# First product copied inside PSUM and the second added to it by TensorE, in a Strassen-Winograd feed-forward stage

## The reference

```python
def reference(x, ctx_1024, g_xattn, g_ffn, Wq, bq, Wk, bk, W_up, W_gate, W_down):
    # _layernorm: (x - mean) / sqrt(var + 1e-5)
    query = einsum('bnc,dc->bnd', ctx_1024, Wq) + bq
    key = einsum('bnc,dc->bnd', ctx_1024, Wk) + bk
    attention = softmax(einsum('bnd,bmd->bnm', query, key))
    x = x + tanh(g_xattn[0]) * einsum('bln,bmn->blm', _layernorm(x), attention)
    # ternary(w): s = mean(|w|) + 1e-8; clip(round(w / s), -1, 1) * s
    wu, wg, wd = ternary(W_up), ternary(W_gate), ternary(W_down)
    n = _layernorm(x)
    hidden = silu(einsum('bsd,ed->bse', n, wu)) * einsum('bsd,ed->bse', n, wg)
    return x + tanh(g_ffn[0]) * einsum('bse,de->bsd', hidden, wd)
```

## Time and profile before

| what | value |
|---|---|
| median of 3 runs | 394.66 us (394.34 to 394.94) |
| span of the profiled execution | 393.2 us |
| median less that span | 1.46 us |
| granted TensorE clock, mean of the span | 1.000 |
| PE busy | 388.2 us (99%), 2000 matmuls |
| DVE busy | 330.2 us (84%) |
| ACT busy | 269.8 us (69%) |
| POOL busy | 183.9 us (47%) |

### The profile page before, as it was taken

One profiled execution on the slowest core, in us unless ns is written; L12 is line 12 of the kernel. 1 busy time (PEld: TensorE's weight loads), 2 busy tenths in 40 slices (PEclk: granted clock), 3 DMA queues, 4 the chain that ended last, 5 costly groups with the idle time before them and its releaser, 6 DMA issues.

```text
span 393.2 us, 6214 instructions
## 1 busy us (share of the span) xinstructions
PE 388.2 (99%) x2000; PEld 219.3 (56%) x2000; DVE 330.2 (84%) x501; ACT 269.8 (69%) x366; POOL 183.9 (47%) x199
## 2 busy tenths in 40 slices
PE   8999999999999999999999999999999999999997
PEld 6676775554444444444444444556545665656886
DVE  0778897988799975789888979999999989798974
ACT  3887988899777786869897982856287566564400
POOL 0498727767845031403169462643639447261000
DMA  8999977799600030020029470006230000000014
GB/s 287 404 402 407 408 232 184 176 261 183 160 2 0 1 108 0 13 96 0 2 60 190 86 148 2 0 1 214 78 139 0 2 1 2 0 2 1 2 61 154
DMA packets 44048, 43.91 MB, mean 112 GB/s; under 512 B 30833, under 2 KB 33009, under 8 KB 42993
## 3 DMA queue, kind: packets, MB, share of 16 engines
q1 hardware_dynamic: 44016, 43.53, 36.3%
HBM read 29.89 MB, written 6.29 MB: 92 GB/s over the span
## 4 chain that ended last, share of the span: by engine, by line
PE 84%; DVE 6%; ACT 4%; issue 4%; DMA 1%; POOL 1%; DVEq 0%; ACTq 0%; POOLq 0%
PE pair L924 20%; PE pair L926 20%; PE pair L1052 14%; PE pair L1000 8%; PE pair L815 7%; PE pair L838 6%; PE pair L788 4%; PE pair L772 3%; PE pair L799 2%; DVE x_sb L1855 1%; DVE xf L1804 1%; DMA xf<-in_first 1%; PE pair L853 1%; DVE sh L1814 1%; ACT xf L1395 1%
## 5 line engine op out<-in xcount | busy, mean ns | idle before, releaser
L924 PE MATMUL pair<-xb_hi,w_sb 128*128 128x512 f16 x448 | 169.8, 379 | 0.9 <-DVE xf L1799 0.5
L926 PE MATMUL pair<-xb_lo,w_sb 128*128 128x512 f16 x448 | 169.8, 379 | 0.0
L924 PEld LDWEIGHTS pair<-xb_hi,w_sb 128*128 128x128 fp8e4 x448 | 43.8, 98 | 54.0 <-DVE xf L1799 1.3
L926 PEld LDWEIGHTS pair<-xb_lo,w_sb 128*128 128x128 fp8e4 x448 | 43.8, 98 | 49.5 <-issue 0.3
L1344 ACT ACTIVATE xf<-xf,small 128x512 f32<-128x512 f32 x48 | 34.5, 720 | 43.5 <-DVE xf L1799 23.6
L1804 DVE SCALAR_TENSOR_TENSOR xf<-xf,small 128x512 f32<-128x512 f32 x48 | 41.7, 870 | 8.5 <-ACT xf L1344 8.4
L1855 DVE SCALAR_TENSOR_TENSOR x_sb<-pair,small,x_sb 128x256 f32<-128x256 f32 (+1 forms) x85 | 37.4, 472 | 6.3 <-PE pair L1052 5.8
L1000 PE MATMUL pair<-x_sb,sh 128*128 128x512 bf16 x192 | 42.4, 379 | 0.0
L626 POOL TENSOR_TENSOR w_sb<-w_sb 128x512 fp8e4<-128x512 fp8e4 x8 | 8.8, 1101 | 55.1 <-ACT w_sb L1215 55.1
L1000 PEld LDWEIGHTS pair<-x_sb,sh 128*128 128x128 f16 x192 | 18.8, 98 | 22.6 <-DVE x_sb L1839 0.2
L1809 DVE TENSOR_TENSOR sh<-xf,sh 128x512 f16<-128x512 f32 x34 | 30.6, 906 | 0.9 <-ACT sh L1357 0.8
(11 more groups left out here) (207 smaller groups left out, 769.2 us busy)
## 6 DMA issues: line engine op xcount, KB each, us to landing
w_sb<-in_wugT SPq DMA_DIRECT2D x8, 1024.0 KB, 14.9
x_sb<-in_x SPq DMA_DIRECT2D x4, 1024.0 KB, 12.8
xf<-in_wdT SPq DMA_DIRECT2D x4, 1024.0 KB, 7.5
xt_sb<-in_wdT SPq DMA_DIRECT2D x4, 1024.0 KB, 4.9
xt_sb<-in_xT SPq DMA_DIRECT2D x12, 256.0 KB, 5.8
x_dram<-x_sb SPq DMA_DIRECT2D x8, 256.0 KB, 3.5
out<-x_sb SPq DMA_DIRECT2D x8, 256.0 KB, 4.2
x_sb<-x_dram SPq DMA_DIRECT2D x4, 512.0 KB, 3.9
```

The lines of the kernel that those rows point to most:

```text
L924: pe.matmul(dst[:, m * 512:(m + 1) * 512], w[:, o:o + P], hi[:, k], start=start and k == 0, stop=False, skip_group_check=not start)
L926: last = pe.matmul(dst[:, m * 512:(m + 1) * 512], w[:, o:o + P], lo[:, k], start=False, stop=k == 1, skip_group_check=not start)
```

## The change

- Product 2 no longer starts a fresh accumulation in ps_y. ScalarE's copy_1 writes product 1 from ps_c into ps_y, and product 2 accumulates on it. add_11 is gone, with its semaphore.
- silu of block 11 reads the up half from ps_y, and make_h of block 11 reads the gate half from ps_y. The waits for block 11's buffer move from copy_1 to silu; copy_1 waits for make_h of block 11 of the tile before, the last reader of ps_y.
- Product 2 now waits for copy_1 of its own tile. It moves behind product 4 of the tile before in tiles 1 to 8, 11 and 12; in tiles 9, 10 and 13 to 15 behind b1 and b5 of its own tile.
- TensorE's order around tiles 9 to 12 changes: 5, 4, 1 in place of 2, 4, 5, 1 behind tile 8; b4(10) stands directly behind b2(10), and product 4(10) behind products 5 and 1 of tile 11.
- ScalarE: copy_1 goes ahead of silu of block 22, silu of block 11 behind silu of block 21 of the tile before, copy_u2 behind a high part; around tile 11 the order is new.
- VectorE: low_h of block 21 and add_12 change places in tiles 0 to 6; evictions and multiplications are reordered in tiles 9 to 13.

The diff, with context lines and a few small hunks (semaphore lists, removed calls of add_11) cut:

```diff
--- before.py
+++ after.py
@@ -99,7 +99,7 @@
         w8 = w_sb[:, :].bitcast(F8).rearrange("p (u m c) -> p u m c", u=NU, m=2)
-        cbuf = {"11": [xf[:, 0:1024]], "12": [xf[:, 1024:2048]],
+        cbuf = {"11": [xf[:, 0:512]], "12": [xf[:, 1024:2048]],
                 "22": [xf[:, 2048:3072], xf[:, 3072:4096]], "21": [c21[:, :]]}
@@ -948,11 +948,8 @@
             def product2(n):
-                if n == 0:
-                    pe.wait_ge(s_exp, NG)
-                else:
-                    pe.wait_ge(s_c["11"], n)
-                product(n, 2, ps_y, A12, "B21", True)
+                pe.wait_ge(s_cp1, n + 1)
+                product(n, 2, ps_y, A12, "B21", False)
 
@@ -1014,8 +1011,8 @@
             product1(0)
+            product5(0)
             product2(0)
-            product5(0)
             for n in range(G0):
@@ -1023,16 +1020,15 @@
                 product1(n + 1)
-                product2(n + 1)
                 product5(n + 1)
                 product4(n)
+                product2(n + 1)
             product6(G0)
...
             product7(G0)
-            product2(G0 + 1)
+            product5(G0 + 1)
             product4(G0)
-            product5(G0 + 1)
             product1(G0 + 1)
@@ -1079,6 +1075,7 @@
                 between_two(n, 5)
+                product2(n)
                 product6(n)
@@ -1086,23 +1083,25 @@
                 between_two(n, 2)
-                product4(n)
-                between_two(n, 4)
-                product2(n + 1)
                 if n == G0 + 1:
+                    product4(n)
+                    between_two(n, 4)
                     product5(n + 1)
...
                 else:
+                    between_two(n, 4)
+                    product5(n + 1)
                     product1(n + 1)
-                    product5(n + 1)
+                    product4(n)
+                    product2(n + 1)
             n = G1 - 1
...
             product7(n)
-            product2(n + 1)
-            product4(n)
             product1(n + 1)
             product5(n + 1)
+            product4(n)
+            product2(n + 1)
             for n in range(G1, NN):
@@ -1113,11 +1112,11 @@
                 else:
-                    product2(n)
                     product5(n)
...
                     between(n, 5)
+                    product2(n)
                     product6(n)
@@ -1136,7 +1135,7 @@
                 final(1, 5, t, ends, True, False)
-            pe.wait_ge(s_c["11"], NN)
+            pe.wait_ge(s_mul["11"], NN)
             pe.wait_ge(s_ef, 14 * NT)
@@ -1336,6 +1335,15 @@
                     src = ps_c[n % 2][:, 0:512]
+                elif c == "11":
+                    act.wait_ge(s_p[2], n + 1)
+                    if n == 0:
+                        act.wait_ge(s_tl, t_done(0, "T2"))
+                    else:
+                        act.wait_ge(s_lo["11"], n)
+                    if n > GB:
+                        act.wait_ge(s_sh["S3"], n - GB)
+                    src = ps_y[:, 0:512]
                 else:
@@ -1365,12 +1373,10 @@
                 if n == 0:
-                    act.wait_ge(s_tl, t_done(0, "T2"))
-                else:
-                    act.wait_ge(s_lo["11"], n)
-                if n > GB:
-                    act.wait_ge(s_sh["S3"], n - GB)
-                act.activation(cb(n, "11"), ps_c[n % 2][:, :], ACT.Copy).then_inc(s_cp1, 1)
+                    act.wait_ge(s_exp, NG)
+                else:
+                    act.wait_ge(s_mul["11"], n)
+                act.activation(ps_y[:, :], ps_c[n % 2][:, :], ACT.Copy).then_inc(s_cp1, 1)
 
@@ -1418,25 +1424,24 @@
             sign_part(2, 0)
+            copy_1(0)
             act.wait_ge(s_t4, 1)
-            copy_1(0)
             act.wait_ge(s_tl, t_done(0, "T3"))
...
             copy_5(0)
-            copy_u2(0)
-            silu(0, "11")
             for n in range(G0 + 1):
...
                     silu(n - 1, "21")
-                    copy_u2(n)
+                silu(n, "11")
+                if n > 0:
+                    high_h(n - 1, "21")
+                copy_u2(n)
                 if n == 7:
...
                     high_s(n - 1, "S1")
-                if n > 0:
-                    high_h(n - 1, "21")
                 if n > GB:
@@ -1489,6 +1494,8 @@
                     sign_down(3)
+                if n < G0:
+                    copy_1(n + 1)
                 silu(n, "22")
@@ -1499,18 +1506,12 @@
                     break
-                copy_1(n + 1)
+                copy_5(n + 1)
                 if not down:
...
                     high_t(NU, "B21", xf_half(2, 1))
-                if n == 1:
-                    copy_5(n + 1)
-                    silu(n + 1, "11")
-                else:
-                    silu(n + 1, "11")
-                    copy_5(n + 1)
             for n in (G0 + 1, G0 + 2):
@@ -1521,10 +1522,10 @@
                     high_s(n - 1, "S1")
+                    copy_5(n)
                     high_h(n - 1, "21")
+                    copy_1(n)
                     high_s(n - 1, "S2")
-                    copy_5(n)
-                    copy_1(n)
                 high_s(n - 1, "S4")
@@ -1538,30 +1539,30 @@
             n = G1 - 1
+            copy_5(n)
+            copy_1(n)
+            high_h(n - 1, "22")
             silu(n - 1, "21")
-            copy_1(n)
-            copy_5(n)
             silu(n, "11")
-            high_h(n - 1, "22")
+            high_s(n - 1, "S1")
             copy_u2(n)
-            high_s(n - 1, "S1")
+            high_h(n - 1, "21")
             high_s(n - 1, "S2")
-            high_h(n - 1, "21")
             silu(n, "12")
...
             high_s(n - 1, "S4")
+            copy_1(n + 1)
             silu(n, "22")
...
             shift(3, 0)
+            copy_5(n + 1)
             silu(n, "21")
-            copy_1(n + 1)
             high_s(n, "S1")
-            copy_5(n + 1)
             high_s(n, "S2")
+            silu(n + 1, "11")
             high_s(n, "S3")
-            silu(n + 1, "11")
+            high_h(n, "21")
             high_s(n, "S4")
-            high_h(n, "21")
             for n in range(G1, NN):
@@ -1783,11 +1784,6 @@
 
-            def add_11(n):
-                dve.wait_ge(s_p[2], n + 1)
-                hold(dve, s_cp1, n + 1)
-                dve.tensor_tensor(cb(n, "11"), ps_y[:, :], cb(n, "11"), ALU.add).then_inc(s_c["11"], 1)
-
             def add_12(n):
@@ -1800,7 +1796,7 @@
                 hold(dve, s_silu[c], n + 1)
-                gate = ps_c[n % 2][:, 512:1024] if c == "21" else cb(n, c)[:, 512:1024]
+                gate = {"21": ps_c[n % 2], "11": ps_y}.get(c, cb(n, c))[:, 512:1024]
                 dve.scalar_tensor_tensor(cb(n, c)[:, 0:512], cb(n, c)[:, 0:512], kap[:, :], gate,
@@ -1882,9 +1877,9 @@
                 make_h(n, "11")
-                add_12(n)
                 if n > 0:
                     low_h(n - 1, "21")
+                add_12(n)
                 if not down:
@@ -1911,7 +1906,6 @@
                 make_h(n, "22")
-                add_11(n + 1)
                 if not down:
@@ -1978,11 +1971,10 @@
             low_s(n - 1, "S1")
-            add_11(n)
             evict_two(n, 1)
+            low_h(n - 1, "21")
             evict_two(n, 5)
             make_h(n, "11")
-            low_h(n - 1, "21")
             add_12(n)
@@ -2000,10 +1992,9 @@
             low_s(n - 1, "S2")
-            add_11(n)
             evict_two(n, 1)
+            evict_two(n, 5)
             make_h(n, "11")
-            evict_two(n, 5)
             add_12(n)
@@ -2011,16 +2002,15 @@
             evict_two(n, 7)
+            evict_two(n, 2)
             make_h(n, "22")
-            evict_two(n, 2)
+            evict_two(n, 4)
             n = G1 - 1
+            weights_1(0)
+            low_h(n - 1, "22")
             make_h(n - 1, "21")
-            evict_two(n - 1, 4)
-            weights_1(0)
-            add_11(n)
+            make_h(n, "11")
             weights_t2(0)
-            make_h(n, "11")
-            low_h(n - 1, "22")
             weights_t4(0)
@@ -2041,13 +2030,13 @@
                     low_s(n - 1, "S2")
-                    add_11(n)
-                final_evict(0, 1, t)
-                if n == G1:
+                    final_evict(0, 1, t)
+                    final_evict(0, 5, t)
+                    make_h(n, "11")
+                else:
+                    make_h(n, "11")
                     low_s(n - 1, "S2")
-                make_h(n, "11")
-                if n > G1:
-                    final_evict(0, 5, t)
+                    final_evict(0, 1, t)
                 add_12(n)
```

4 lines of the change are left out of this document (1 added, 3 removed).

## The result

The changed kernel takes 404.42 us (median of 5 runs, 403.03 to 404.94), the kernel before 394.59 in the runs beside it (393.90 to 394.94, 5 runs): ratio 1.0245, 95% interval 1.0230 to 1.0259, or 9.8 us slower. The forecast was 400.7 and the range ended at 403.7: the sign was right, the size was not.

The account below looks back on a forecast made before the run. TensorE, busy 99% of the span, bounds the kernel. Late starts 0.06 + 0.8 + 2.05 + 2.07 + 1.4 + 1.8 = 8.2 us less today's 2.1 give +6.0; 394.66 + 6.0 = 400.7 us, range 396.0 to 403.7.

Parts of the forecast that it names:

- step 1: Tiles 5 and 7: product 4 waits for add_22, 0.45 and 0.35 us late, sum 0.8 us.
- step 2: Piece b1(9) waits for make_h(8, 21): 2.05 us, against 0.35 before the change; the largest step.
- step 3: Tile 9 up to product 1(10), which waits for the first half's evictions: 2.07 us late in all, against 0.94 before.
- step 4: Piece b4(10) waits for the two evictions of b7(10): 1.4 us late, new.
- step 5: Products 1(13), 1(14), 1(15) wait for the eviction of b4 of the tile before: 1.3, 0.24, 0.24 us, sum 1.8.
- Three waits that were to go: Late starts forecast to vanish: 0.30 us before 3(8), 0.08 before 1(11), 0.42 before 6(12).
- The copy: ScalarE's copy_1, PSUM to PSUM, taken as 1.02 us; product 2 has 0.5 us reserve, 0.3 in tile 9; cost nothing.
- The rival of a dear copy: A PSUM write of 2.0 us makes product 2 late in tiles 9 to 11, 13 to 15: 403.7 us, chance 0.05.
- Relief of VectorE: Rival: 19.5 us less VectorE work and shorter make_h close steps 3 to 5: 395.4 us, chance 0.10.
- The failed step: ScalarE's queue: silu of block 11 and a high part end before product 6 drains, so copy_u2 isn't delayed; cost nothing.
- new short waits of 0.3 us in some ten places: Allowance for unforeseen waits in the upper end of the range: + 3 us.
- The device time around the span: Time outside the profiled span: span 393.2 us, taken as 1.46 us under the median of the runs shown.

## Why the prediction was right in sign and too small

- **"So the change is a matter of waits"** held to a tenth of a microsecond: the stage is longer by 9.05, the late starts by 9.05. In the experiments on the changed kernel, too, stage and waits moved together.
- **Steps 1 to 5** held: 0.45 and 0.51 (0.86 forecast), 1.95 (2.05), 2.16 (2.07), 1.40 (1.4), 2.03 (1.8). With the order alone, in the kernel before, b4(10) was 1.39 late at its own place (step 4), and a lost product cost 1.69 close to that of step 2, before 4(8). Steps 1, 3 and 5 had no run of their own; what speaks for them is that the wait stands at the forecast place, has the forecast size and is ended by the forecast instruction. Three waits that were to go went.
- **The copy.** 1.02 us was taken for it, it takes 1.01 (median of 16), and no product 2 waits for it; doubled, it costs where the reserve said. The rival of a dear copy is out. (Its own terms, five times 0.5 and 0.7, add up to 3.2 us and not to 3.0.)
- **Relief of VectorE.** 18.0 us went from VectorE's total, and no forecast wait came out more than 0.1 us shorter than its forecast. 19.5 and more were to go: the multiplications lost another 2.8 us (53.6 to 50.8), but the low parts at L1805 took 2.6 more (49.8 to 52.4), held up by GpSimd in new places.
- **The failed step** is "ScalarE is free for copy_u2, for which product 7 waits. Cost nothing". It counted silu and high part from the drain of product 4 as if the high part were ready when ScalarE reached it. The high part needs make_h of block 21, and that stands in VectorE's queue behind a multiplication and two low parts; I looked at ScalarE's queue and not at what the instruction ahead of the copy itself waits for. The price is 1.2 us directly, at 7(1) and 7(2). The swapped order gave back 1.9: another 0.7 at dh2(7) and 1(8), which hung on the 0.1 us that decided which low part came first, less 0.1 at 4(7).
- **Behind it stands a second fault:** no step asked which of VectorE's instructions GpSimd would hold up in the new order. The low parts of the kernel before (L1809) take 684 ns in the median but up to 2018. In the places that cost time they took 1.4 to 1.7 us.
- **A step that was missing:** VectorE's new order in tile 12 was in the diff, and no cost was worked out for it. It cost 1.0 us at b6(12), 0.65 net.
- **The range** allowed 3 us for "new short waits of 0.3 us in some ten places". They were four of 0.15, 0.44, 1.01 and 1.09, 2.7 us in all. With the 6.0 forecast and 0.3 us of sizes this makes 9.05; the last 0.8 lie between the profiled execution and the median and stay open, with the wait before 7(1) as the likely part.
- **The device time around the span** was taken as 1.46 us from a median and a span of different executions. Where both are listed for one execution it is 1.8 (403.03 and 401.2). That enters both kernels alike.

What was not tried: the changed order of TensorE throughout with VectorE's sum kept. So how much the accumulation gives back against the same order with a sum is open; only product 2(9) was moved that way.

## What to carry to other kernels

Accumulating on a copy makes one product wait for another of its own group. The product that had freedom of place, and so covered other waits, can then stand in few places. Before such a change list for each wait how much matmul work lies between its cause and it, in the old and the new order; here this gave every forecast wait to 0.25 us.

Then do the same for the engines that feed it: when an instruction is put behind another, ask what that other one waits for, through the next queue too, and where GpSimd runs beside VectorE, ask which of the two starts first and use the long durations of the line, not its median.
